# Both cross attentions regrouped: one tile of 128 queries at a time, probabilities packed end to end, next tile's scores issued first

## The chip, the cores and the metric

One kernel runs on one core of a Trainium2 chip. The metric is device time in microseconds (us), the median of several runs. The core's engines work in parallel, each through its own list of instructions in order, and wait for each other by semaphores: TensorE (PE; PEld are its weight loads), VectorE (DVE), ScalarE (ACT), GpSimd (POOL) and SyncE (SP, which issues transfers).

## The reference

Six blocks run in a row on 2048 tokens of 256 features (8 batches of 256), each followed by a residual and a layer norm: windowed self attention, cross attention, a routed feed-forward block, a recurrence, a second cross attention, a feed-forward block with binarized weights. The change touches the two cross attentions, which compute, for 16 heads of 16 features and 77 context rows per batch:

```
Q = proj(query, Wq, bq); K = proj(key, Wk, bk); V = proj(value, Wv, bv)
scores = jnp.einsum('bhqd,bhkd->bhqk', Q, K) / np.sqrt(D_K)
scores = jnp.where(m == 0, NEG, scores)      # the first; the second adds a mask
attn = jax.nn.softmax(scores, axis=-1)
x = jnp.einsum('bhqk,bhkd->bhqd', attn, V)
return x.transpose(0, 2, 1, 3).reshape(b, -1, D_MODEL) @ Wo.T + bo
```

## The kernel before, in words

`cross_attention` is called twice. The first call ("additive" false) gets an integer mask and the second ("additive" true) one to be added. A batch is two tiles of 128 queries, and a tile is cut into four units of four heads, so a batch has eight units. A loop in which each engine writes out its order by hand runs over the batches; the function `batch` of each engine is that order.

A unit goes through these steps. `score` (TensorE, L1200) is one f32 product of queries with a block of masked keys `ca_km`, 308 wide (4 heads x 77). `mask_scores` (VectorE, L1076 in the first call, L1074 in the second) writes the masked scores to `ca_z`. `take_maximum` (VectorE, L1082) finds the row maxima, `subtract` (GpSimd, L953) takes them off, `power` (ScalarE, L1017) is one exponential over 308. `turn_probs` (TensorE, L1209) transposes four blocks of 77, the copy to `ca_pth` (ScalarE, L1025) and `probs_rest` to `ca_ptl` (VectorE, L1087) split them into a high and a low f16 part. `weigh` (TensorE, L1223) is 12 small f16 products with the values, whose last column is the sum of the probabilities.

VectorE masks and reduces unit c+2 while it makes the low part of unit c, and ScalarE's exponential is for unit c+1. So three units are under way at once, each in one of two buffers:

```
L1110  two_on = (b, c + 2) if c < UNITS - 2 else (b + 1, c + 2 - UNITS) if after else None
L1112      mask_scores(*two_on)
L1113  probs_rest(b, c)
L1115      take_maximum(*two_on)
```

The other work of a batch (token transposes, the query, key and value projections of the next batch, head transposes, the output projection "mix") goes through two shared PSUM banks in a fixed ring, `CA`; its list of slots says after which unit each step stands. The 77 keys are masked by head on GpSimd (L947).

Of the kernel before, what the change touches and what calls it, by code (L numbers as in the profile page):

```python
# [209 lines left out]
def window_attention(nc, x_dram, xt_dram, wqkv_dram, wo_dram, rope_dram, ident, half, X, next_loads):  # L210
    with ExitStack() as ctx:
# [562 lines left out]
UH = 4  # L774
UNITS = TPB * CH // UH
MASKED = -4.0e9
OPEN = 1.0e38
CA = Ring(
    steps=[
        [("key", 0)],  # L780
        [("value", 0)],
        [("heads", 1)],
        [("mix", 1)],
        [("tokens", 0)],
        [("query", 0)],
        [("heads", 0)],
        [("mix", 0)],
    ],
# [6 lines left out]
class CrossWeights:  # L795


    def __init__(self, ctx, nc, tag, additive):
        self.tag, self.additive = tag, additive

        def sb(name, shape, dt=F32):
            return ctx.enter_context(nc.sbuf_tensor(f"{tag}_{name}", shape, dt))

        self.w = sb("w", [P, 4, KT_, DIM])
        self.bias = sb("bias", [P, 2, KT_])
        self.rows = sb("rows", [P, 2, DIM])
        self.mask = sb("mask", [P, TILES, CTX], F32 if additive else I32)
        self.loaded = ctx.enter_context(nc.semaphore(f"{tag}_loaded"))

    def load(self, sp, w_dram, b_dram, rows_dram, mask_dram):  # L810
        for tile, dram in ((self.bias, b_dram), (self.rows, rows_dram), (self.w, w_dram), (self.mask, mask_dram)):
# [3 lines left out]
def cross_attention(nc, weights, ctx_dram, ident, half, X, next_loads=None, table=None):  # L815
    tag, additive = weights.tag, weights.additive
    w, bias, rows, mask = weights.w, weights.bias, weights.rows, weights.mask
    with ExitStack() as ctx:
# [9 lines left out]
        context = [sb(f"context{k}", [P, KT_, CTX]) for k in range(2)]  # L828
        xs = [sb(f"xs{k}", [P, TPB, DIM]) for k in range(2)]
        limit = None if additive else sb("limit", [P, TILES, CTX])  # L830
        head_of = sb("head_of", [P, CH // KT_])
        xt = [sb(f"xt{k}", [P, KT_, SEQ]) for k in range(2)]
        q = [sb(f"q{k}", [P, KT_, SEQ]) for k in range(2)]
        kb = sb("kb", [P, KT_, CTX])
        km = [sb(f"km{k}", [P, KT_, CH // KT_, CTX]) for k in range(2)]
        v = sb("v", [P, CH, CD])
        vh = [sb(f"vh{k}", [P, CH, CD + 1], F16) for k in range(2)]
        vl = [sb(f"vl{k}", [P, CH, CD + 1], F16) for k in range(2)]
        z = [sb(f"z{k}", [P, UH, CTX]) for k in range(2)]
        top = sb("top", [P, 2, UH])  # L840
        probs = [sb(f"probs{k}", [P, UH, CTX]) for k in range(2)]
        pth = [sb(f"pth{k}", [P, UH * P], F16) for k in range(2)]
        ptl = [sb(f"ptl{k}", [P, UH * P], F16) for k in range(2)]
# [3 lines left out]
        xb = sb("xb", [P, TPB, DIM])  # L847

        shared = [ctx.enter_context(nc.psum_tensor(f"{tag}_shared{k}", [P, 512], F32)) for k in range(2)]
        s_bank = [ctx.enter_context(nc.psum_tensor(f"{tag}_scores{k}", [P, 512], F32)) for k in range(2)]  # L850
        t_bank = [ctx.enter_context(nc.psum_tensor(f"{tag}_turned{k}", [P, 512], F32)) for k in range(2)]
        o_bank = [ctx.enter_context(nc.psum_tensor(f"{tag}_out{k}", [P, CH, 32], F32)) for k in range(2)]
# [5 lines left out]
        limits = sem("limits")  # L858
        ones = sem("ones")
        full = [sem("full0"), sem("full1")]  # L860
        free = [sem("free0"), sem("free1")]
        key_masked = sem("key_masked")
# [11 lines left out]
        weighted = sem("weighted")  # L874
        inverted = sem("inverted")
        normed = sem("normed")
# [18 lines left out]

        block_scope = ExitStack()
# [3 lines left out]
        def _(sp):  # L900
            def load_context(b, par):
                sp.dma_start(context[par][:], ctx_dram[:, :, bass.ds(b * CTX, CTX)]).then_inc(context_loaded[par], 16)
# [28 lines left out]
        def _(pool):  # L931
# [8 lines left out]
            pool.wait_ge(consts, 3)  # L940
            if table:
                table.prepare(pool)
            pool.wait_ge(weights.loaded, 64)

            def mask_keys(b, par, g):
                wait_read(pool, [("key", 0)], b)
                pool.tensor_tensor(km[par][:, g], kb[:, g].unsqueeze(1).broadcast_to((P, CH // KT_, CTX)),  # L947
                                   head_of[:].unsqueeze(2).broadcast_to((P, CH // KT_, CTX)), ALU.mult).then_inc(key_masked, 1)
# [1880 lines left out]
```

## Time and profile before

| what | value |
|---|---|
| runs | 1293.85 us median of 3 (1289.38 to 1293.98) |
| profiled execution | 1291.09 us, of which the span of the core is 1289.3 us |
| mean granted TensorE clock | 0.924 of full speed |
| PE, DVE, ACT, POOL busy | 84%, 75%, 55%, 30% of the span |
| first cross attention | about 421 to 591.5 us of the span |
| second cross attention | about 1042 to 1207.7 us |

Busy time is a share of an engine's own time; PE's is modelled and its instructions overlap, so a busy PE isn't one at its peak. An idle time in square brackets on a row names what the engine waited for. A granted clock of 1.00 is 2.4 GHz, 0.50 is 1.2 GHz, and a mean between them is a stretch with some of both.

### The profile page before, as it was taken

What the parts mean: (1) busy time and instruction counts of PE and PEld (TensorE: products, weight loads), DVE (VectorE), ACT (ScalarE), POOL (GpSimd) and SP (SyncE); (2) the same over time, 40 slices, a digit from 0 to 9 for tenths busy, and PEclk for the clock granted to TensorE, in tenths of its full rate; (3) what the DMA queues carried; (4) which work ended last, traced back from release to release, by engine and by line L of the source; (5) the groups of instructions that cost most, each with busy time, mean ns of one, the idle gap of its engine ahead of it and who ended that gap; (6) DMA issues with size and microseconds to landing.
All of it is one profiled execution on the core that took longest, in us unless ns stands there. A gap on an engine that the chain in (4) does not pass through costs nothing. (4 is left out here: it accounts for less than half of the span.)

```text
span 1289.3 us, 30260 instructions
## 1 busy us (share of the span) xinstructions
PE 1087.8 (84%) x10763; PEld 881.4 (68%) x10763; DVE 961.6 (75%) x2254; ACT 704.9 (55%) x1459; POOL 388.9 (30%) x538
## 2 busy tenths in 40 slices
PE   4899989999987699986269999389999569999696
PEld 3578878778776577774257777378787447777485
DVE  7587877878875488884938883569998538888497
ACT  2454444444443355552637775368788525655484
POOL 5122222222220355551130000423331225555232
PEclk9899999999999799995559999699999879999799
DMA  6000000100000500005245431300000000000011
GB/s 257 5 10 2 10 12 2 71 3 2 2 2 2 187 23 22 11 9 227 107 135 172 171 108 49 120 17 26 24 9 9 0 24 23 11 21 9 34 50 50
DMA packets 34072, 65.35 MB, mean 51 GB/s; under 512 B 7590, under 2 KB 23334, under 8 KB 30886
## 3 DMA queue, kind: packets, MB, share of 16 engines
q1 hardware_dynamic: 32422, 59.62, 13.2%
q0 software_dynamic: 1536, 4.20, 1.0%
q8 instruction: 73, 1.20, 0.4%
q14 instruction: 41, 0.34, 0.1%
HBM read 43.03 MB, written 12.39 MB: 43 GB/s over the span
## 5 line engine op out<-in xcount | busy, mean ns | idle before, releaser
L953 POOL TENSOR_TENSOR ca_z<-ca_z,ca_top 128x308 f32<-128x308 f32 x128 | 92.7, 724 | 129.8 <-DVE ca_top L1082 129.5
L389 ACT ACTIVATE wa_probs<-wa_scores,wa_minus_top 128x192 f32<-128x192 f32 x256 | 83.3, 437 | 80.6 <-DVE wa_minus_top L477 80.6
L1025 ACT ACTIVATE ca_pth<-ca_turned 77x512 f16<-77x512 f32 x128 | 75.9, 593 | 59.0 <-PE ca_turned L1209 58.4
L348 POOL TENSOR_TENSOR wa_q<-wa_by_cos,wa_by_sin 128x256 f32<-128x256 f32 x32 | 23.4, 732 | 266.3 <-DVE wa_by_sin L472 266.3
L1209 PE MATMUL ca_turned<-ident,ca_probs 128*77 128x128 f32 x512 | 84.1, 287 | 20.6 <-ACT ca_probs L1017 19.5
L400 ACT ACTIVATE wa_pth<-wa_turned 128x384 f16<-128x384 f32 x128 | 58.4, 506 | 73.5 <-PE wa_turned L696 73.5
L1200 PE MATMUL ca_scores<-ca_km,ca_q 128*128 128x308 f32 x256 | 89.6, 433 | 6.0 <-ACT ca_q L998 5.7
L1087 DVE SCALAR_TENSOR_TENSOR ca_ptl<-ca_turned,ca_pth 77x512 f16<-77x512 f32 x128 | 86.7, 677 | 2.6 <-ACT ca_pth L1025 2.6
L1017 ACT ACTIVATE ca_probs<-ca_z 128x308 f32<-128x308 f32 x128 | 58.2, 455 | 44.8 <-POOL ca_z L953 43.8
L621 PE MATMUL wa_scores<-wa_xh,wa_wh 128*128 128x256 f16 x256 | 70.5, 275 | 11.7 <-DVE wa_wl L456 9.7
L477 DVE TENSOR_REDUCE wa_minus_top<-wa_scores 128x2 f32<-128x384 f32 x128 | 62.3, 549 | 21.1 <-PE wa_scores L684 18.9
L696 PE MATMUL wa_turned<-ident,wa_probs 128*128 128x128 f32 x512 | 69.1, 277 | 9.4 <-DVE wa_ptl L525 5.4
L1209 PEld LDWEIGHTS ca_turned<-ident,ca_probs 128*77 128x77 f32 x512 | 56.0, 148 | 26.4 <-ACT ca_probs L1017 22.6
L525 DVE SCALAR_TENSOR_TENSOR wa_ptl<-wa_turned,wa_pth 128x384 f16<-128x384 f32 x128 | 65.0, 549 | 8.6 <-ACT wa_pth L400 8.6
L2385 PE MATMUL re_g<-re_convh,re_w_gh 128*128 128x256 f16 x256 | 69.8, 273 | 1.2 <-DVE re_convl L2280 1.2
L621 PE MATMUL wa_scores<-wa_xl,wa_wh 128*128 128x256 f16 x256 | 70.5, 275 | 0.0
L621 PE MATMUL wa_scores<-wa_xh,wa_wl 128*128 128x256 f16 x256 | 70.4, 275 | 0.0
L2385 PE MATMUL re_g<-re_convl,re_w_gh 128*128 128x256 f16 x256 | 69.8, 273 | 0.0
L2385 PE MATMUL re_g<-re_convh,re_w_gl 128*128 128x256 f16 x256 | 69.8, 273 | 0.0
L696 PEld LDWEIGHTS wa_turned<-ident,wa_probs 128*128 128x128 f32 x512 | 58.1, 142 | 16.4 <-issue 7.5
L2369 PE MATMUL re_in<-re_xt,re_w_in 128*128 128x256 f32 x256 | 61.6, 402 | 9.0 <-ACT re_xt L2150 9.0
L2369 PEld LDWEIGHTS re_in<-re_xt,re_w_in 128*128 128x128 f32 x256 | 51.0, 202 | 18.8 <-issue 7.2
(332 smaller groups left out, 3677.0 us busy)
## 6 DMA issues: line engine op xcount, KB each, us to landing
ex_stage<-in_ew SPq DMA_DIRECT2D x16, 1024.0 KB, 7.0
slots<-slots_zeros SPq DMA_DIRECT2D x10, 512.0 KB, 5.3
ca_xs<-tokens SPq DMA_DIRECT2D x16, 256.0 KB, 2.3
ex_xe<-slots SPq DMA_DIRECT2D x11, 320.0 KB, 3.3
slots<-ex_y SPq DMA_DIRECT2D x9, 320.0 KB
wa_x_stage<-in_xt SPq DMA_DIRECT2D x8, 256.0 KB, 3.0
tokens<-in_x SPq DMA_DIRECT2D x1, 2048.0 KB, 14.8
ca_w<-in_xw SPq DMA_DIRECT2D x2, 1024.0 KB, 5.6
```

The lines of the kernel that those rows point to most:

```text
L389: ins = act.activation(probs[2 * (u % 2) + t][:, h, t * WINDOW:t * WINDOW + SPAN], s_bank[i][:, t * SPAN:(t + 1) * SPAN], ACT.Exp, bias=mi ...
L477: dve.tensor_reduce(minus_top[:, g % 2, i], s_bank[i][:, 0:2 * SPAN].rearrange("p (t s) -> p t s", t=2), AX.X, ALU.max, negate=True).then_ ...
L525: dve.scalar_tensor_tensor(out=spans(ptl[k][:]), in0=spans(t_bank[h][:]), scalar=PSCALE, in1=spans(pth[k][:]), op0=ALU.mult, op1=ALU.subtr ...
L621: ins = pe.matmul(bank[:, a * SEQ:(a + 1) * SEQ], weight[:, k, cols], x[:, par, k], start=(m == 0), stop=(m == 3 * KT_ - 1))
L696: ins = pe.transpose(t_bank[h][:, j * SEQ + t * P:j * SEQ + (t + 1) * P], probs[2 * (u % 2) + t][:, h, j * P:(j + 1) * P], ident[:])
L953: pool.tensor_tensor(z[k][:], z[k][:], top[:, k].unsqueeze(2).broadcast_to((P, UH, CTX)), ALU.subtract).then_inc(shift, 1)
L1025: act.activation(pth[k][0:CTX], t_bank[k][0:CTX], ACT.Copy, scale=PSCALE).then_inc(probs_high, 1)
L1087: dve.scalar_tensor_tensor(out=ptl[k][0:CTX], in0=t_bank[k][0:CTX], scalar=PSCALE, in1=pth[k][0:CTX], op0=ALU.mult, op1=ALU.subtract).then ...
L1200: pe.matmul(s_bank[c % 2][:, 0:UH * CTX], q[par][:, g, t * P:(t + 1) * P], km[par][:, g, h:h + UH].rearrange("p h k -> p (h k)"), start=Tr ...
L1209: ins = pe.transpose(t_bank[k][0:CTX, h * P:(h + 1) * P], probs[k][:, h], ident[:])
L2369: ins = pe.matmul(i_bank[s % 2][:, k], w_in[:, g, m * P:(m + 1) * P], xt[:, g], start=(g == 0), stop=(g == KT_ - 1))
L2385: ins = pe.matmul(g_bank[m][:, k], w[:, j, cols], x[par][:, j], start=(n == 0), stop=(n == 3 * HT - 1))
```

## The change

A unit of work becomes a tile of 128 queries: all 16 heads' scores stand in four PSUM banks at once (four heads in each). The 16 x 77 = 1232 probabilities of a query are written end to end (`ca_probs`, 1280 wide) and turned in ten blocks of 128 in three sets (4, 4 and 2 blocks), so that a block holds parts of two or three heads. The values are laid out to fit: 25 entries of a block and a head, each masked by a table `owner`, so the value projection is 20 products over blocks of 128 context rows (the context is given three times in a row). `weigh` is 30 products into one shared bank. The keys are not masked by head on GpSimd any more: ScalarE writes each 16-feature half in turn (L1038, four copies of 77), and the score products use 32 rows of the array each (8 products, 154 wide). In the first call the mask enters on TensorE by four bf16 products with an identity (L1306); in the second VectorE adds it. The largest score is subtracted by VectorE (first call) or GpSimd (second) for banks 0 and 1 only; for banks 2 and 3 ScalarE subtracts it as a bias, in four exponentials of 77 each.

Each engine's `batch` is now a loop over two tiles. `nxt` is the next tile, whose scores and exponentials are worked on while the present tile is turned. The core of the diff:

```diff
 # ScalarE
+                for t in range(TPB):
+                    nxt = ahead(b, t, after)
+                    if t == 0:
+                        slot(0, b, par)
+                    high(b, t, 0)
+                    if nxt:
+                        power(*nxt, 0)
+                    slot(6 if t else 1, b, par)
+                    high(b, t, 1)
+                    if nxt:
+                        power(*nxt, 1)
+                    if t == 0:
+                        slot(2, b, par)
+                    high(b, t, 2)
+                    if nxt:
+                        power(*nxt, 2)
+                    if t == 0:
+                        slot(3, b, par)
+                    elif after:
+                        value_high(b + 1, 1 - par)
+                    if nxt:
+                        power(*nxt, 3)
...
+            def power(b, t, r):
+                if r < SUBTRACTED:
+                    act.wait_ge(shift, SUBTRACTED * tile + r + 1)
+                    act.activation(out, z[r][:], ACT.Exp).then_inc(exped, 1)
+                else:
+                    act.wait_ge(maxed, UNITS * tile + r + 1)
+                    for h in range(UH):
+                        ins = act.activation(out[:, h], src[:, h], ACT.Exp, bias=minus_top[:, t, r, h:h + 1])
...
 # VectorE
+                for t in range(TPB):
+                    if t == 1:
                         normalise(b, 0)
+                    elif before:
                         normalise(b - 1, 1)
+                    if before:
+                        norm.apply(dve, b - 1, t, at(X, (b - 1) * TPB + t))
+                    low(b, t, 0)
+                    if nxt:
+                        softmax(*nxt, 0)
+                    low(b, t, 1)
+                    if nxt:
+                        softmax(*nxt, 1)
+                    if t == 1:
+                        slot(7, b, par)
+                    low(b, t, 2)
+                    if nxt:
+                        softmax(*nxt, 2)
+                        softmax(*nxt, 3)
+                    if t == 1 and after:
                         value_low(b + 1, 1 - par)
+                    slot(8 if t else 4, b, par)
...
+            def softmax(b, t, r):
+                dve.wait_ge(scores, tile + 1)
+                if additive:
+                    dve.tensor_tensor(z[r][:], s, m, ALU.add).then_inc(masked, 1)
+                dve.tensor_reduce(minus_top[:, t, r], z[r][:] if additive else s, AX.X, ALU.max, negate=True).then_inc(maxed, 1)
+                if r < SUBTRACTED and not additive:
+                    dve.tensor_tensor(z[r][:], s, minus_top[:, t, r].unsqueeze(2).broadcast_to((P, UH, CTX)),
+                                      ALU.add).then_inc(shift, 1)
...
 # TensorE
+            def score(b, t, par):
+                if not (first(b) and t == 0):
+                    pe.wait_ge(masked if additive else exped, UNITS * tile)
...
+                for t in range(TPB):
+                    if nxt:
+                        score(*nxt, par if t == 0 else 1 - par)
+                    if t == 0:
+                        slot(0, b, par)
+                    turn(b, t, 0)
+                    slot(6 if t else 1, b, par)
+                    turn(b, t, 1)
+                    slot(7 if t else 2, b, par)
+                    turn(b, t, 2)
+                    if t == 0:
+                        slot(3, b, par)
+                    slot(8 if t else 4, b, par)
+                    slot(9 if t else 5, b, par)
```

The slots of the ring are: 0 tokens, 1 heads 1 (of the batch before), 2 query, 3 key, 4 mix 1 (of the batch before), 5 weigh 0, 6 heads 0, 7 value, 8 mix 0, 9 weigh 1. Tokens, query, key and value serve the next batch. A step waits until the bank of the step two before it is read, so weigh 0 waits for ScalarE's key copy.

Two places of the order in the first call's loop follow. `ca_pth` and `ca_ptl` are the high and low parts, `ca_ot` turned heads, `ca_q` queries, `ca_xt` turned tokens; REGISTER_ALU and ISA rows are loop counters.

ScalarE, in the middle of a batch, before:

```order
L1025 ACTIVATE ca_pth<-ca_turned 77x512
L1014 REGISTER_ALU
L1017 ACTIVATE ca_probs<-ca_z 128x308
L993 REGISTER_ALU
L995 ACTIVATE ca_xt<-ca_shared 128x512
L1025 ACTIVATE ca_pth<-ca_turned 77x512
L1014 REGISTER_ALU
L1017 ACTIVATE ca_probs<-ca_z 128x308
L998 ACTIVATE ca_q<-ca_shared,ca_bias 128x256 x2
```

The same engine at the start of tile 0 now:

```order
L1074 ACTIVATE ca_pth<-ca_turned 128x512
L1059 ISA
L1060 ACTIVATE ca_probs<-ca_z 128x308
L1041 ACTIVATE ca_ot<-ca_shared 128x256
L1071 REGISTER_ALU
L1074 ACTIVATE ca_pth<-ca_turned 128x512
L1059 REGISTER_ALU
L1060 ACTIVATE ca_probs<-ca_z 128x308
L1028 REGISTER_ALU
L1033 ACTIVATE ca_q<-ca_shared,ca_q_bias 128x256 x2
L1071 REGISTER_ALU
L1074 ACTIVATE ca_pth<-ca_turned 128x256
```

VectorE in the same place, before:

```order
L1076 TENSOR_TENSOR ca_z<-ca_scores,ca_limit 128x308
L1087 SCALAR_TENSOR_TENSOR ca_ptl<-ca_turned,ca_pth 77x512
L1082 TENSOR_REDUCE ca_top<-ca_z 128x4
L1062 SCALAR_TENSOR_TENSOR ca_vl<-ca_v,ca_vh 77x16x16
L1076 TENSOR_TENSOR ca_z<-ca_scores,ca_limit 128x308
L1087 SCALAR_TENSOR_TENSOR ca_ptl<-ca_turned,ca_pth 77x512
L1082 TENSOR_REDUCE ca_top<-ca_z 128x4
```

And VectorE now:

```order
L1167 SCALAR_TENSOR_TENSOR ca_ptl<-ca_turned,ca_pth 128x512
L1147 ISA
L1155 TENSOR_REDUCE ca_minus_top<-ca_scores 128x4
L1158 ISA
L1159 REGISTER_ALU
L1160 TENSOR_TENSOR ca_z<-ca_scores,ca_minus_top 128x308
L1166 REGISTER_ALU
L1167 SCALAR_TENSOR_TENSOR ca_ptl<-ca_turned,ca_pth 128x512
L1155 TENSOR_REDUCE ca_minus_top<-ca_scores 128x4
L1158 REGISTER_ALU
L1159 REGISTER_ALU
L1160 TENSOR_TENSOR ca_z<-ca_scores,ca_minus_top 128x308
```

Where the exponential of one unit stood between the high parts of two others, whose maxima had been made an engine's turn earlier, it now stands between two sets of the same tile, and needs the reduction and the subtraction that stand between the same two sets on VectorE.

TensorE, where the value projection stands, before (`ca_turned` are the transposes):

```order
L1209 MATMUL ca_turned<-ident,ca_probs 77x128 x4
L1200 MATMUL ca_scores<-ca_km,ca_q 128x308
L1179 MATMUL ca_shared<-ca_w,ca_context 77x256 x2
L1218 ISA
L1223 MATMUL ca_out<-ca_vh,ca_pth 128x17
```

And in tile 1 now:

```order
L1324 MATMUL ca_turned<-ident,ca_probs 128x128 x4
L1276 MATMUL ca_shared<-ca_w,ca_context 128x32 x2
L1276 MATMUL ca_shared<-ca_w,ca_context 128x48 x2
L1276 MATMUL ca_shared<-ca_w,ca_context 128x32 x2
L1276 MATMUL ca_shared<-ca_w,ca_context 128x48 x4
L1276 MATMUL ca_shared<-ca_w,ca_context 128x32 x2
L1276 MATMUL ca_shared<-ca_w,ca_context 128x48 x4
L1276 MATMUL ca_shared<-ca_w,ca_context 128x32 x4
L1321 REGISTER_ALU
L1324 MATMUL ca_turned<-ident,ca_probs 128x128 x2
```

Two value products became 20, and the turning of a tile's third set stands behind them.

## Rows read from the trace of the kernel before

**Rows 1.** Busy time of each engine by stretch, number of instructions in brackets.
```profile
core 0: us, PE busy (x) PEld busy (x) DVE busy (x) ACT busy (x) POOL busy (x), PEclk, DMA share, GB/s
420.80:591.50 170.70, 146.48 (x1440) 118.64 (x1440) 131.70 (x343) 87.59 (x192) 86.65 (x116) 0.94 0.14 47
462.15:498.87 36.72, 34.79 (x361) 28.62 (x360) 32.65 (x86) 21.92 (x49) 21.32 (x29) 1.00 0.07 21
1060.07:1096.82 36.75, 34.27 (x359) 27.97 (x357) 30.88 (x79) 22.07 (x48) 21.32 (x28) 1.00 0.07 20
```
**Rows 2.** Timeline of VectorE: start, duration, engine, line, operation [idle before].
```profile
462.15 0.41 DVE L1057 TENSOR_TENSOR ca_v<-ca_shared,ca_rows 77x256 f32<-77x256 f32 x1
...
472.15 0.48 DVE L1076 TENSOR_TENSOR ca_z<-ca_scores,ca_limit 128x308 f32<-128x308 f32 x1 [1.34 <-PE ca_scores L1200]
472.55 0.68 DVE L1087 SCALAR_TENSOR_TENSOR ca_ptl<-ca_turned,ca_pth 77x512 f16<-77x512 f32 x1
473.14 0.46 DVE L1082 TENSOR_REDUCE ca_top<-ca_z 128x4 f32<-128x308 f32 x1
473.52 0.46 DVE L1076 TENSOR_TENSOR ca_z<-ca_scores,ca_limit 128x308 f32<-128x308 f32 x1
...
498.87 0.41 DVE L1057 TENSOR_TENSOR ca_v<-ca_shared,ca_rows 77x256 f32<-77x256 f32 x1
```
**Rows 3.** Waits from 462.15 to 535.61 us: total, times, longest.
```profile
DVE ca_z L1076 <- PE ca_scores L1200: 6.8, 8, 1.4
```
**Rows 4.** Timeline, all engines: a unit alone, at the first call's start.
```profile
435.03 0.47 DVE L1082 TENSOR_REDUCE ca_top<-ca_z 128x4 f32<-128x308 f32 x1
...
435.58 0.70 POOL L953 TENSOR_TENSOR ca_z<-ca_z,ca_top 128x308 f32<-128x308 f32 x1 [6.15 <-DVE ca_top L1082]
...
436.31 0.46 ACT L1017 ACTIVATE ca_probs<-ca_z 128x308 f32<-128x308 f32 x1 [3.84 <-POOL ca_z L953]
...
436.83 1.14 PE L1209 MATMUL ca_turned<-ident,ca_probs 128*77 128x128 f32 x4 [3.29 <-ACT ca_probs L1017]
```
**Rows 5.** Timeline of ScalarE in a steady batch.
```profile
467.02 0.60 ACT L995 ACTIVATE ca_xt<-ca_shared 128x512 f32<-128x512 f32 x1
...
470.06 0.84 ACT L998 ACTIVATE ca_q<-ca_shared,ca_bias 128x256 f32<-128x256 f32 x2 [0.49 <-PE ca_shared L1169]
470.84 0.59 ACT L1025 ACTIVATE ca_pth<-ca_turned 77x512 f16<-77x512 f32 x1
471.33 0.45 ACT L1017 ACTIVATE ca_probs<-ca_z 128x308 f32<-128x308 f32 x1
472.15 0.39 ACT L1005 ACTIVATE ca_ot<-ca_shared 128x256 f32<-128x256 f32 x1 [0.38 <-PE ca_shared L1184]
...
477.16 0.54 ACT L1003 ACTIVATE ca_kb<-ca_shared,ca_bias 128x77 f32<-128x77 f32 x2 [0.51 <-PE ca_shared L1175]
```
**Rows 6.** Timeline of TensorE: window attention, then weight loads and transposes of a cross batch.
```profile
300.00 0.81 PE L678 MATMUL wa_scores<-wa_band,wa_ident_bf 128*128 128x384 bf16 x4
300.75 1.58 PE L684 MATMUL wa_scores<-wa_k,wa_q 32*128 32x192 f32 x32
302.26 0.20 PE L714 MATMUL wa_out<-wa_vh,wa_pth 128*128 128x65 f16 x1
...
302.97 0.19 PE L714 MATMUL wa_out<-wa_vh,wa_ptl 128*128 128x65 f16 x1
...
475.77 1.12 PEld L1175 LDWEIGHTS ca_shared<-ca_context,ca_w 128*128 128x128 f32 x8
...
479.35 0.64 PE L1209 MATMUL ca_turned<-ident,ca_probs 128*77 128x128 f32 x4
```
**Rows 7.** Stretches of 3 us at the starts of both calls, columns as in rows 1.
```profile
433.00:436.00 3.00, 0.54 (x3) 0.05 (x1) 2.86 (x6) 0.00 (x0) 0.42 (x1) 0.84 1.09 385
436.00:439.00 3.00, 2.17 (x8) 1.81 (x8) 0.39 (x1) 1.40 (x3) 0.98 (x2) 0.50 1.09 385
...
1054.00:1057.00 3.00, 1.33 (x10) 1.20 (x10) 1.31 (x4) 1.17 (x4) 1.40 (x2) 1.00 0.00 0
```

More of the change, by code:

```diff
@@ L773 @@
 CH, CD = 16, 16
[L774 to L777, printed above, removed]
+UNITS = 4
+UH = CH // UNITS
+ROWS_T = CH * CTX
+CHUNKS = -(-ROWS_T // P)
+FLAT = CHUNKS * P
+SETS = [(0, 4), (4, 8), (8, CHUNKS)]
+PAIR = 2 * CTX
+SUBTRACTED = 2
+MASKED = -1.0e30
+TOUCHED = [(P * c // CTX, min(P * (c + 1) - 1, ROWS_T - 1) // CTX + 1) for c in range(CHUNKS)]
+ENTRY = [sum(z - a for a, z in TOUCHED[:c]) for c in range(CHUNKS)]
+ENTRIES = sum(z - a for a, z in TOUCHED)
+ORDER = [8 * g + 2 * r + j for r in range(UNITS) for g in range(KT_) for j in range(2)]
 CA = Ring(
     steps=[
+        [("tokens", 0)],
+        [("heads", 1)],
+        [("query", 0)],
         [("key", 0)],
+        [("mix", 1)],
+        [("weigh", 0)],
+        [("heads", 0)],
         [("value", 0)],
[L782 to L786, printed above, removed]
         [("mix", 0)],
+        [("weigh", 1)],
     ],
@@ L894, in both, with ahead @@
             return run
+        def ahead(b, t, after):
+            return (b, 1) if t == 0 else (b + 1, 0) if after else None
         block_scope = ExitStack()
@@ L1019, in batch @@
[L1019 to L1033 removed]
+                act.wait_ge(v_masked, b + 1)
@@ L1106, in residual, with slot @@
                 norm.statistics(dve, b, t)
[L1108 to L1116 removed]
+            def slot(s, b, par):
+                for kind, i, bank, uses in CA.slot(s, b):
+                    if kind == "value":
+                        value(b + 1, 1 - par, bank, uses)
+                    if kind == "mix":
+                        residual(b + CA.serves(kind, i), i, bank, uses)
@@ L1117, in batch @@
+            def batch(b, par, before=True, after=True):
+                for t in range(TPB):
+                    nxt = ahead(b, t, after)
+                    if t == 1:
                         normalise(b, 0)
-                    if c == 1 and before:
+                    elif before:
                         normalise(b - 1, 1)
-                    for kind, i, bank, uses in CA.slot(c, b):
-                        if kind == "value":
-                            value(b + 1, 1 - par, bank, uses)
-                        if kind == "mix":
-                            residual(b + CA.serves(kind, i), i, bank, uses)
@@ new lines, in turn @@
+            def turn(b, t, i):
+                n = 6 * b + 3 * t + i
+                pe.wait_ge(exped, UNITS * (b * TPB + t) + (2 if i == 0 else UNITS))
+                if not (first(b) and 3 * t + i < 2):
+                    pe.wait_ge(probs_low, n - 1)
+                a, e = SETS[i]
+                for c in range(a, e):
+                    ins = pe.transpose(t_bank[(3 * t + i) % 2][:, (c - a) * P:(c - a + 1) * P], probs[t][:, c * P:(c + 1) * P], ident[:])
+                ins.then_inc(probs_t, 1)
```

392 lines of the change are left out of this document (199 added, 193 removed).

## The prediction

> **What bounds the kernel now.** I read the busy times by stretch first. A steady stretch of two batches of either call, 36.7 us, has the clock at 1.00, and no engine but VectorE and TensorE is over 60% busy [rows 1]. The timeline of VectorE then shows the period: the same instruction (the value copy, L1057) starts at 462.15 and, two batches on, at 498.87, so a batch takes 18.36 us [rows 2]. Within it a unit's three VectorE steps start 0.40, 0.59 and 0.38 us apart, 1.37 us for mask, low part and maximum; the reader is to see that they follow each other without a gap, since each serves another unit. Eight units are 11.0 us of the 18.4; the rest is norms, copies and 1.7 us a batch of waiting for scores (6.8 us in four batches [rows 3]). So VectorE bounds both calls, and everything else runs beside it.
>
> The other view is one unit alone, at the start, where nothing overlaps [rows 4]: maximum, subtraction, exponential, transposes, each begun 0.03 to 0.08 us after the one before has ended. Before the change that chain is hidden by the three units under way. I call such a step a hand-off and take 0.05 us.
>
> **What the change takes off VectorE.** In the first call, per tile, four masks (0.40 each) go, two subtractions come (0.48, with 0.04 of waiting for the maximum ahead), and the low parts fall from four of 512 to two of 512 and one of 256 (0.60 + 0.60 + 0.33 = 1.53 for 2.4). Per tile 4 x 1.37 = 5.5 becomes two maxima with subtraction (2 x 0.89), two without (2 x 0.38) and 1.53: 4.1. In the second call each maximum must wait for its own add right ahead of it (0.52 + 0.38), so 4 x 0.90 + 1.53 = 5.1. With the wait for scores gone too, VectorE alone would allow 18.36 - 1.7 - 2.8 = 13.9 and 18.36 - 1.7 - 0.8 = 15.9 us a batch. That is the gain on offer: 4.5 and 2.5 us a batch.
>
> **What the change adds: a chain between ScalarE and VectorE.** Both engines take their lists in order. ScalarE's list reads: high part of set 0, exponential 0 of the next tile, high part of set 1, exponential 1, high part of set 2, exponentials 2 and 3. VectorE's reads: low part 0, maximum 0 (and subtraction), low part 1, maximum 1, low part 2, maxima 2 and 3. Low part 0 needs high part 0; maximum 0 stands behind low part 0; exponential 0 needs maximum 0; high part 1 stands behind exponential 0; and so on. While one works the other waits, where before every step's input had been made a unit earlier. I add up one tile from the end of high part 0 to the same point of the next tile. Durations: copy of 512 starts its follower 0.49 after it and lasts 0.59, exponential of 308 0.45, query copies 0.74 to the next start, head copy 0.30 to the next (0.39 long), token copy 0.52, two copies of 77 with a bias 0.54, so 0.22 apart and 0.32 long [rows 5]. Four pieces of 77 are then 0.98, or 0.88 to the next start; a 256-wide f16 copy I take as the 256-wide head copy, 0.38.
>
> First call. Round 0: hand-off 0.05, low 0.60, maximum 0.46 and 0.04, subtraction 0.48, hand-off 0.05, exponential 0.45, head copy 0.30, high part 0.59: 3.0. Round 1: the same with high part 0.38 and no head copy, 2.5, in tile 0 with the query copies 3.25. Round 2: 0.05, low 0.33, maximum 0.46, 0.05, pieces 0.88, key copies 0.88 (tile 0) or value copy 0.45 (tile 1), pieces 0.98: 3.65 and 3.2. Then the turn-round, since here the next scores wait for the last exponential, and the transposes stand behind the scores. A score step is four bf16 products of 308 (four of 384 start 0.16 apart, so 0.13 each) and 16 short-row products (8 f32 ones, each shown as two; 32 of 192 wide take 1.58, 0.04 each): 0.52 + 0.64 and 0.3 until the last is out, 1.46, of which the transposes wait for 1.2 [rows 6]. Transposes 0.64, hand-off, high part 0.59: with the score a little late behind weigh 0 it is 2.6 after tile 0; after tile 1, where the token transposes (0.65) and their copy (0.52) come first, 3.1. Tile 0 is 12.5, tile 1 is 11.8.
>
> In tile 1 the value projection stands ahead of set 2's transposes: 20 products, 40 weight loads. Eight such loads take 1.12, 0.13 apart [rows 6], so 5.2 us for what took four. It starts about when high part 0 ends, so high part 2 ends at 5.2 + 0.40 + 0.05 + 0.38 = 6.0 where the rounds alone give 5.5: 0.4 more. A batch of the first call is 24.7 us, 6.3 over 18.36.
>
> Second call. Rounds 0 and 1 have the add (0.52) and GpSimd's subtraction (0.70 [rows 4], 0.72 with hand-off part) in place of VectorE's subtraction: 3.8 and 3.3 (4.0 with the query). Round 2: 4.15 and 3.7. The next scores wait only for the adds, and so run early. But weigh 0 (30 f16 products at 0.03 [rows 6], 0.93) waits for the key copies, and scores (0.64) and transposes (0.64) stand behind it: 2.0. After tile 1 the token transposes wait for the residual, behind the value's low part on VectorE: 1.85. Tiles 14.0 and 12.65; a batch 26.6, 8.3 over 18.36.
>
> **The sum.** Seven batch periods lie within each call: 7 x 6.3 = 44 and 7 x 8.3 = 58. At the ends, the first value projection has 36 more loads ahead of the first scores (36 x 0.13 = 4.7, up to 8 at half clock), the context transfer is three times as large, and the last tile lacks a next tile's rounds; I take +2 a call, between -3 and +8. That is +106.
>
> The rest is TensorE's clock. In tile 0, after the key projection, TensorE has only the mix products (about 1 us) until the key copies: by the rounds above it is silent for some 2.4 and 2.0 us in the first call, 3.1 and 2.5 in the second. At the first call's start it was silent for 3.29 us [rows 4], and the granted clock fell to 0.84 and 0.50 in those stretches; in the stretch of 1054 us, with 1.33 us of work in three, it stayed at 1.00 [rows 7]. So it may fall in some batches. At half rate the pieces on the chain cost themselves once more: 1.2 + 0.64 + 0.9 = 2.7 us a batch in the first call, 0.93 + 0.64 + 0.64 = 2.2 in the second, and some 2 for the value projection. Nothing in any batch is 0, all batches of both calls 7 x (2.7 + 2.2 + 2) = 48; I take 10, since only the second call's silences come near 3.29.
>
> The profiled execution took 1291.1 us (span 1289.3 and 1.8 around it), 2.8 below the median of the runs. 1291 + 106 + 10 = 1407.
>
> The Trainium skill ("TensorE: Matmul & The Clock Gate", section "What's actually happening") says that the default state is throttled and that activity releases the throttle. By that rule a stage with such holes would lose the clock in every batch, and the sum would be 1445; the row of 1054 us speaks against counting on it. The same skill ("TensorEngine Tiling (Array Packing)", section "Key Properties") says that a change of tiling mode drains the engine, which speaks against short-row products twice a batch. The trace shows the first of them 0.27 us after the last full-height product started at 0.16 us a step [rows 6]; by the rule with that number it is 0.11 x 4 a batch at most, already within the 0.3 above.
>
> **Rivals.** (a) The same chain, and the clock falls in nearly every batch: 1291 + 106 + 48 = 1445. For it: the holes; against it: the row of 1054 us. (b) The pieces of the chain are cheaper than the rows of before allow to see, above all ScalarE's exponentials of 77 and the copies beside them, so that half of the excess goes: 1291 + 53 + 10 = 1354. For it: those shapes have no row of their own; against it: 0.22 apart is what copies with a bias show. (c) Faster: VectorE stays the bound. It decides from where ScalarE's high parts and exponentials are ready before VectorE reaches them, so that the rounds overlap; then 7 x (4.5 + 2.5) = 49 goes and some 6 comes at the ends, 1248. For it: VectorE has the largest share now and is given less to do; against it: the order of the two lists, which leaves no step that could be early. (d) No net change: in the first call VectorE bounds (-32), in the second half of the excess comes (+29): 1288. That the four exponentials run at all and the sets are as wide as said is in the order.
>
> **How the numbers follow.** The forecast has 0.62, (a) 0.18, (b) 0.10, (c) 0.06, (d) 0.04. A difference under 0.5% can't be told from none here. Faster 0.06, same 0.04, slower 0.90. The range goes from 1350, just past (b), to 1445, which takes in (a); what lies outside is (c), (d) and the tails, some 0.15. The likeliest case's own range is 1385 to 1425.
>
> **What would show it.** The period between value copies on VectorE: 24.7 and 26.6 us a batch. ScalarE idle before its exponentials, released by VectorE's (second call: GpSimd's) subtraction, and VectorE idle before its low parts, released by ScalarE's high part, about 0.6 us and more each, six or so times a tile; VectorE under 65% busy in both calls. The value projection about 5 us at the full clock. The prediction is wrong if VectorE has no idle time before its low parts, if the period is under 21 us, or if the time is gained back outside both calls, where nothing changes.

## The result, and the profile after

| | time, us | ratio to before (95% interval) | profiled execution | clock |
|---|---|---|---|---|
| before | 1293.91 median of 4 | | 1291.09 | 0.924 |
| after | 1454.1 median of 4 (1453.88 to 1459.07) | 1.1243 (1.1190 to 1.1296) | 1453.88, span 1451.9 | 0.849 |

12% slower. The direction and the mechanism came out as forecast, the size did not: 1454 against 1407, 9 us above the upper end of the range. All of the difference but 2.6 us lies in the two cross attentions. From the first context transfer to the last residual they took 167.4 and 164.1 us before and take 241.3 and 250.2 now, +160.0.

First the counterpart of [rows 1]: a batch of the first call and one of the second, from value copy to value copy (us, busy us and instructions of each engine, granted clock, DMA share, GB/s).

```profile
529.92:557.24 27.32, 20.96 (x194) 17.07 (x193) 13.97 (x38) 11.73 (x36) 3.89 (x7) 0.81 0.06 18
1253.02:1282.94 29.92, 22.10 (x182) 19.17 (x181) 15.83 (x41) 12.27 (x36) 6.78 (x10) 0.69 0.05 17
```

Five of the six steady batches of the first call take 27.3 us and one 25.9 (mean 27.1), instead of 18.36 [rows 2]; in the second call the six take 29.4 in the mean (28.1 to 32.1). VectorE is busy 51 to 53% of a batch, where it had 84 to 89%, and the clock, at 1.00 in [rows 1], is 0.81 and 0.69.

The waits of two batches (529.92 to 584.56), the counterpart of [rows 3], and of two of the second call (1253.02 to 1311.07): engine and line, what it waited for, us in total, times, longest.

```profile
DVE ca_ptl L1167 <- ACT ca_pth L1074: 18.2, 12, 2.4
...
ACT ca_probs L1060 <- DVE ca_z L1160: 13.2, 8, 1.7
```

```profile
ACT ca_probs L1060 <- POOL ca_z L979: 19.8, 8, 2.8
DVE ca_ptl L1167 <- ACT ca_pth L1074: 19.1, 11, 2.3
```

These are the two sides of the alternation: VectorE waits before all twelve low parts for ScalarE's high part, and ScalarE before all eight whole exponentials for the subtraction. VectorE's timeline in one tile shows it [idle before, and for whom]:

```profile
566.12 0.69 DVE L1167 SCALAR_TENSOR_TENSOR ca_ptl<-ca_turned,ca_pth 128x512 f16<-128x512 f32 x1 [2.29 <-ACT ca_pth L1074]
566.72 0.47 DVE L1155 TENSOR_REDUCE ca_minus_top<-ca_scores 128x4 f32<-128x308 f32 x1
567.23 0.48 DVE L1160 TENSOR_TENSOR ca_z<-ca_scores,ca_minus_top 128x308 f32<-128x308 f32 x1
568.99 0.69 DVE L1167 SCALAR_TENSOR_TENSOR ca_ptl<-ca_turned,ca_pth 128x512 f16<-128x512 f32 x1 [1.28 <-ACT ca_pth L1074]
...
572.11 0.42 DVE L1167 SCALAR_TENSOR_TENSOR ca_ptl<-ca_turned,ca_pth 128x256 f16<-128x256 f32 x1 [1.53 <-ACT ca_pth L1074]
```

From one low part to the next is 2.87 and 3.12 us; round 0 was forecast at 3.0 and round 1 with the query at 3.25. The reader sees rounds of the forecast length, in batches that are 2.6 us too long. The rest stands in the clock. Stretches of 2 us of the same tile (PE's busy time is the second number, the clock the third from the end):

```profile
558.00:560.00 2.00, 1.21 (x32) 0.83 (x30) 1.20 (x3) 1.12 (x6) 0.91 (x1) 1.00 0.46 118
560.00:562.00 2.00, 0.65 (x3) 0.41 (x4) 1.51 (x5) 1.22 (x5) 0.00 (x0) 0.87 0.00 0
562.00:564.00 2.00, 2.00 (x19) 1.29 (x18) 1.65 (x4) 0.00 (x0) 1.43 (x3) 0.50 0.00 0
564.00:566.00 2.00, 2.00 (x15) 2.00 (x15) 0.00 (x0) 1.11 (x2) 0.00 (x0) 0.78 0.00 0
...
570.00:572.00 2.00, 0.14 (x1) 0.15 (x1) 0.55 (x2) 1.39 (x4) 0.00 (x0) 0.93 0.00 0
572.00:574.00 2.00, 1.93 (x4) 1.02 (x4) 1.23 (x4) 1.12 (x6) 0.00 (x0) 0.50 0.00 0
```

The clock falls twice in the batch: at 561, after the weighing of tile 1, and at 572, after the key projection. TensorE's timeline shows what then runs at half rate:

```profile
561.35 1.11 PE L1306 MATMUL ca_scores<-ca_mask_now,ca_ident_bf 128*128 128x308 bf16 x4 [1.82 <-ACT ca_probs L1065]
562.40 1.41 PE L1312 MATMUL ca_scores<-ca_km,ca_q 32*128 32x154 f32 x16
563.73 1.11 PE L1258 MATMUL ca_shared<-ident,ca_xs 128*128 128x128 f32 x4
...
571.86 2.07 PE L1288 MATMUL ca_shared<-ca_w,ca_ot 128*128 128x256 f32 x4 [2.21 <-ACT ca_q L1033]
```

At full clock (e1_fill below) the first three take 0.69, 0.81 and 0.66, the last 1.03 to 1.13. So the batch spends 1.5 us more before the next high part 0 and 1.0 more before the weighing, 2.5 of the 2.6 us.

At the first call's start, the counterpart of [rows 7], the value projection is the long row, and the clock is 0.50 although TensorE is shown busy without a break:

```profile
425.07 1.96 PE L1270 MATMUL ca_shared<-ca_context,ca_w 128*128 128x77 f32 x8 [6.63 <-DMA ca_context<-in_context]
426.82 8.66 PE L1276 MATMUL ca_shared<-ca_w,ca_context 128*128 128x32 f32 x40
```

```profile
427.00:430.00 3.00, 3.00 (x17) 3.00 (x16) 0.00 (x0) 1.33 (x4) 0.00 (x0) 0.50 1.08 385
430.00:433.00 3.00, 3.00 (x16) 3.00 (x16) 0.00 (x0) 0.00 (x0) 0.00 (x0) 0.50 1.08 382
```

### The profile page after: what moved, and what is told of

The parts are those of the page before. It is cut to its first block and busy times, and to the rows that moved or that the text cites. A ratio compares the mean times of both kernels' runs of the same rounds, so it can differ in the third digit from the quotient of the medians.

```text
span 1451.9 us, 30374 instructions
## 1 busy us (share of the span) xinstructions
PE 1162.0 (80%) x10891; PEld 951.6 (66%) x10891; DVE 944.9 (65%) x2201; ACT 721.8 (50%) x1651; POOL 300.1 (21%) x444
## 5 line engine op out<-in xcount | busy, mean ns | idle before, releaser
L1167 DVE SCALAR_TENSOR_TENSOR ca_ptl<-ca_turned,ca_pth 128x512 f16<-128x512 f32 (+1 forms) x96 | 57.6, 602 | 149.1 <-ACT ca_pth L1074 149.1
L1060 ACT ACTIVATE ca_probs<-ca_z 128x308 f32<-128x308 f32 x64 | 29.4, 460 | 130.2 <-POOL ca_z L979 73.4
L1276 PEld LDWEIGHTS ca_shared<-ca_w,ca_context 128*128 128x128 f32 x640 | 93.2, 236 | 0.0
L1276 PE MATMUL ca_shared<-ca_w,ca_context 128*128 128x32 f32 (+1 forms) x640 | 92.9, 313 | 0.0
L1288 PE MATMUL ca_shared<-ca_w,ca_ot 128*128 128x256 f32 x128 | 52.4, 552 | 34.8 <-ACT ca_q L1033 30.2
L1074 ACT ACTIVATE ca_pth<-ca_turned 128x512 f16<-128x512 f32 (+1 forms) x96 | 49.8, 520 | 58.0 <-PE ca_turned L1324 58.0
L1246 PEld LDWEIGHTS ca_shared<-ca_vh,ca_pth 128*128 128x128 f16 x320 | 31.9, 109 | 54.3 <-issue 37.0
L1246 PE MATMUL ca_shared<-ca_vh,ca_pth 128*128 128x34 f16 (+1 forms) x320 | 35.1, 200 | 40.0 <-ACT ca_km L1038 22.5
```

Source lines behind the costliest of these rows:

```text
L1167: dve.scalar_tensor_tensor(out=ptl[t][:, a * P:e * P], in0=t_bank[(3 * t + i) % 2][:, 0:(e - a) * P], scalar=PSCALE, in1=pth[t][:, a * P:e ...
L1246: ins = pe.matmul(out, p[:, cols], x[:, ENTRY[c]:ENTRY[c] + e - a].rearrange("p e d -> p (e d)"), start=(c == 0 and n == 0), stop=(c == CH ...
L1276: ins = pe.matmul(dst[:, ENTRY[c] * CD:(ENTRY[c] + e - a) * CD], context[par][:, k, key:key + P], w[:, 2, k, a * CD:e * CD], start=(k == 0 ...
L1288: ins = pe.matmul(dst[:, 0:DIM], ot[:, i, g], w[:, 3, g], start=(g == 0), stop=(g == KT_ - 1))
```

## The experiments

Calls are measured from the first context transfer to the last residual, batches between value copies (mean of the six behind the first interval), both in the profiled execution. The rest of the program takes 957 to 962 us in all kernels but e7.

| kernel | time, us | ratio (95% interval) | calls, us | batch, us |
|---|---|---|---|---|
| after | 1454.1 | 1.1243 (1.119 to 1.130) | 241.3, 250.2 | 27.1, 29.4 |
| e1_fill | 1428.3 | 1.1005 (1.095 to 1.106) | 225.4, 237.0 | 25.0, 27.4 |
| e2_high | 1433.0 | 1.1041 (1.100 to 1.108) | 234.3, 239.4 | 26.9, 27.7 |
| e3_turn | 1448.9 | 1.1164 (1.103 to 1.129) | 238.0, 244.0 | 27.2, 27.6 |
| e4_value | 1470.2 | 1.1328 (1.128 to 1.137) | 248.6, 262.4 | 28.8, 30.8 |
| e5_order | 1297.0 | 1.0008 (0.999 to 1.003) | 166.0, 169.3 | 18.0, 17.9 |
| e6_mixed | 1429.0 | 1.1031 (1.098 to 1.109) | 228.7, 238.9 | 25.5, 27.1 |
| e7_value8 | 1436.8 | 1.1091 (1.104 to 1.115) | 241.6, 249.8 | 27.8, 29.3 |
| e8_shift | 1266.1 | 0.9759 (0.970 to 0.981) | 150.7, 154.6 | 16.7, 17.0 |
| e9_shift_warm | 1271.8 | 0.9815 (0.977 to 0.986) | 150.9, 154.9 | 16.6, 17.0 |
| e10_first8 | 1440.8 | 1.1114 (1.100 to 1.123) | 234.4, 244.1 | 27.1, 29.6 |

**e1_fill: idle transposes in TensorE's holes.**

```diff
+            def fill(n, b, t):
+                pe.wait_ge(probs_low, 6 * b + 3 * t + 2)
+                for _ in range(n):
+                    pe.transpose(t_bank[(3 * t + 1) % 2][:, 0:P], ident[:], ident[:])
 # after the key projection 14, after mix 1 of tile 0 12, after weigh 1 10;
 # 40 once, ahead of the first batch
```

> The changed kernel with idle TensorE transposes of the identity added, into a transpose bank that nothing uses at that moment: 14 after the key projection, 12 after mix 1, 10 after weigh 1 in each batch and 40 before the first batch (0.11 us each at full clock). They add no result. If the excess over the forecast (1454 against 1407) is TensorE's clock, the granted clock in steady batches rises from 0.81 and 0.69 to 0.95 or more, the periods fall from 27.3 and 29.4 us to 24.7 and 26.6 as forecast, and the time to 1400 to 1415. If instead the pieces of the chain between ScalarE and VectorE were sized too small, the clock rises and the periods stay above 26.5 and 28.5: 1440 or more.

1428.3, 26 less than the changed kernel, between the two expectations. Both of the falls seen above went; one at a new place stayed in most batches. The last batch of the first call had none, and the one of 545 did (one stretch is the value projection itself):

```profile
545.90:550.90 5.00, 5.00 (x48) 5.00 (x46) 3.01 (x6) 1.82 (x4) 0.00 (x0) 1.00 0.00 0
550.90:552.90 2.00, 2.00 (x14) 1.39 (x13) 1.68 (x5) 0.98 (x4) 1.03 (x1) 0.51 0.21 25
...
600.50:625.00 24.50, 21.38 (x231) 18.45 (x230) 14.34 (x38) 11.67 (x36) 3.90 (x7) 1.00 0.00 0
```

A batch wholly at full clock takes 24.5 us; 24.7 was forecast. And the clock fell at 551 at the end of 4.55 us of value products, with no idle time on TensorE since 543. The same 4.55 us of products in the last batch left it at 1.00, so they alone do not decide it:

```profile
546.29 4.55 PE L1276 MATMUL ca_shared<-ca_w,ca_context 128*128 128x32 f32 x40
...
620.34 4.55 PE L1276 MATMUL ca_shared<-ca_w,ca_context 128*128 128x32 f32 x40
```

**e2_high: ScalarE makes high part 1 ahead of exponential 0.**

```diff
                     high(b, t, 0)
+                    high(b, t, 1)
                     if nxt:
                         power(*nxt, 0)
                     slot(6 if t else 1, b, par)
-                    high(b, t, 1)
```

> The changed kernel with one swap on ScalarE: the high part of set 1 stands ahead of exponential 0 instead of behind it. If the alternation of ScalarE and VectorE is the chain, this takes the high part (0.59), the exponential (0.45), the head copy (0.30) and two hand-offs out of it, 1.3 to 1.4 us a tile over 32 tiles: 1454 - 43 = 1411, and VectorE's idle time before low part 1 goes. If TensorE's steps (scores, turning, value projection at the low clock) set the period, the time stays within 10 us of 1454.

1433.0, half of the gain expected. In two batches of the first call the wait before low parts fell from 18.2 to 14.0 us and that before exponentials from 13.2 to 6.6, so one hand-off less a tile does what it should; but ScalarE's wait for the transposes rose from 7.1 to 13.1, and the clock takes a share. Two batches of the second call, one after the other:

```profile
1211.60:1236.80 25.20, 18.91 (x186) 16.45 (x186) 15.55 (x40) 12.53 (x36) 6.30 (x9) 0.87 0.03 10
1236.80:1266.40 29.60, 23.49 (x185) 20.97 (x184) 15.77 (x41) 12.62 (x36) 6.29 (x9) 0.71 0.08 26
```

The same instructions in the same order, 4.4 us apart, with the clock at 0.87 and 0.71.

**e3_turn: TensorE turns set 0 ahead of the next tile's scores.**

```diff
+                    turn(b, t, 0)
                     if nxt:
                         score(*nxt, par if t == 0 else 1 - par)
                     if t == 0:
                         slot(0, b, par)
-                    turn(b, t, 0)
```

> The changed kernel with set 0 of a tile turned ahead of the next tile's scores instead of behind them. Chain theory: the high and low part of set 0 (1.2 us) then run beside the scores instead of behind them, and the scores are 1.2 us at the full clock, 2.4 at half: 1 to 2 us a tile in the first call, 0.6 in the second, 16 tiles each: 1454 - 26 to 42, so 1412 to 1428. Rival (the order of the two steps on TensorE does not matter, since the next maxima need the scores in either order): 1447 to 1461.

1448.9 (1442.2, the run that the table's calls are from, and 1455.6); the interval holds the changed kernel's ratio, so no gain can be told. The first call's period stays at 27.2, so the turn-round alone isn't what bounds it there; presumably a high part made earlier meets the same alternation.

**e4_value: the value projection behind set 2's transposes** (VectorE's and ScalarE's value steps moved behind it).

```diff
-                    slot(7 if t else 2, b, par)
+                    if t == 0:
+                        slot(2, b, par)
                     turn(b, t, 2)
+                    if t == 1:
+                        slot(7, b, par)
```

> The changed kernel with the value projection behind set 2's transposes on TensorE, its copy behind maximum 3 on VectorE and the high part of the values behind exponential 3 on ScalarE. The forecast gave the value projection 0.4 us a batch of the first call (8 batches, 3 us) by holding up set 2; the trace of the changed kernel shows set 2's high part beginning right behind exponential 1, so this should bring 0 to 10 us: 1444 to 1454. Rival: 40 weight loads at the low clock (8.6 us) hold up set 2 in every batch; then 2 to 3 us a batch, 1405 to 1425.

1470.2: slower by 16, where both expectations were of no loss. The projection now stands between set 2 and the weighing, the clock of the steady batches is 0.67 to 0.74, and ScalarE's longest wait for transposes is 4.2 us (3.6 without the edit). Where the projection stood it cost less; what of the 16 us is the clock and what the place is not told apart.

**e5_order: the same instructions, another order within the tile, on all four engines.** The lists of three engines for tile 0, in words (GpSimd's and those of tile 1 change too):

```diff
 # ScalarE
-tokens, high 0, exp 0, heads, high 1, exp 1, query, high 2, exp 2, key, exp 3
+high 0, tokens, heads, high 1, key, exp 0, high 2, exp 1, query, exp 2, exp 3
 # VectorE
-norm, apply, low 0, max 0, low 1, max 1, low 2, max 2, max 3, residual
+norm, low 0, max 0, max 1, max 2, low 1, low 2, apply, max 3, residual
 # TensorE
-score, tokens, turn 0, heads, turn 1, query, turn 2, key, mix, weigh
+turn 0, tokens, score, heads, turn 1, key, turn 2, query, mix, weigh
```

> Same instructions on every engine, only their order within a tile is changed, on all four: ScalarE makes the high parts of sets 0 and 1 before the next tile's exponentials, VectorE takes three of the next maxima between its low parts, TensorE turns set 0 first and runs the key projection ahead of the query. Theory (the alternation of the two lists is the excess): VectorE alone needs 13.9 and 15.9 us a batch, TensorE's pieces add up to 17.2 in the first call (value 5.0, scores 2.4, transposes 2.5, mix 1.75, query 1.75, weigh 1.9, key 0.95, tokens and heads 1.0) and 16.0 in the second, so TensorE and VectorE bound it: periods of 17.5 to 18.5 and 16.8 to 17.5 at full clock, 1300 us; with a clock that still falls once a batch 2 to 3 us more, 1340. Rival (the clock, not the order, makes most of the excess): the holes move but stay, 1400 or more. Rival (the rounds' length is in the pieces themselves): periods stay over 24 and the time over 1425.

1297.0, the time of the kernel before: the order of the four lists was worth 157 us, what it spared in falls of the clock included. Two batches of the first call and two of the second, and the wait before low parts in the two from 485.4 to 520.6:

```profile
502.90:538.10 35.20, 33.62 (x386) 28.89 (x385) 27.54 (x72) 23.54 (x72) 8.39 (x14) 1.00 0.09 28
1084.13:1119.83 35.70, 34.48 (x369) 30.45 (x368) 30.81 (x82) 24.42 (x73) 13.37 (x18) 0.88 0.10 31
```

```profile
DVE ca_ptl L1183 <- ACT ca_pth L1081: 2.3, 4, 0.7
```

2.3 us where it was 18.2, and in the first call VectorE 78% and TensorE 96% busy at clock 1.00. TensorE is the engine that is full now. Both rivals fall: at clock 1.00 the old order still takes 24.5 us a batch (e1_fill), the new one 17.6; in the second call the new order takes 17.9 though the clock still falls (0.88). Four lists changed at once, so which swap counts most is not told; one swap on ScalarE alone (e2_high) was worth 21 us, one on TensorE alone (e3_turn) nothing that can be told.

**e6_mixed: e1_fill, with two idle transposes after each of the value projection's last blocks.**

```diff
+                        if c == 2 and not first(b):
+                            pe.wait_ge(probs_low, 6 * b - 2)
+                        if 2 <= c < len(TOUCHED) - 1:
+                            for _ in range(2):
+                                pe.transpose(t_bank[1][:, 0:P], ident[:], ident[:])
```

> The kernel of e1_fill, and beside it two idle transposes after each of the last blocks of the value projection (14 in all, some 1.7 us a batch). In e1_fill the clock still fell once a batch, at the end of the value projection, where TensorE has no idle time in the trace. Theory (a stream of small products behind weight loads lowers the clock by itself): with wide products among them the clock stays at 1.00 in the steady batches, periods are 24.7 plus about 1 in the first call and 26.6 plus 1 in the second, and the time 1415 to 1430, since what the clock gives back the transposes take. Rival (the fall comes from a silence elsewhere): the granted clock of the steady batches stays at 0.9 and the time rises by 14 x 1.7 to about 1450.

The clock stays at 1.00 through all six steady batches of either call; four of each:

```profile
526.30:577.30 51.00, 45.29 (x487) 39.43 (x486) 28.45 (x73) 23.58 (x72) 7.81 (x14) 1.00 0.06 20
577.30:628.20 50.90, 45.18 (x486) 39.35 (x485) 28.44 (x73) 23.57 (x72) 7.83 (x14) 1.00 0.03 10
1181.10:1235.60 54.50, 43.23 (x470) 38.17 (x469) 31.47 (x80) 24.41 (x72) 12.49 (x19) 1.00 0.06 20
1235.60:1290.10 54.50, 43.24 (x470) 38.18 (x469) 31.49 (x80) 24.40 (x72) 12.49 (x19) 1.00 0.06 18
```

Against e1_fill the only edit is inside the value projection, so the unbroken stream of small products had a part in the falls there; that it is not enough by itself the last batch of e1_fill shows. The projection is 1.2 us longer (5.75 for 4.55) and the batch 0.95 longer than e1_fill's at full clock, so the time stays.

**e7_value8: the value projection of batches 1 to 7 in 4 wide products.**

```diff
+                    for lo, hi in () if first(b) else ((0, DIM), (DIM, ENTRIES * CD)):
+                        for k in range(KT_):
+                            ins = pe.matmul(dst[:, lo:hi], context[par][:, k, 0:P], w[:, 2, k, 0:hi - lo],
+                                            start=(k == 0), stop=(k == KT_ - 1))
-                    for c, (a, e) in enumerate(TOUCHED):
+                    for c, (a, e) in enumerate(TOUCHED if first(b) else ()):
```

> The changed kernel with the value projection of batches 1 to 7 done in 4 wide products (8 weight loads, columns 256 and 144) instead of 20 small ones (40 loads); left out is each block's own offset into the context, so the values are not the reference's. The forecast has 0.4 us a batch of the 5.2 us projection on the path at full clock: by that alone 14 x 0.4 = 6, 1448. If the projection also causes the fall of the clock at the end of tile 1, that fall goes, the scores and transposes after tile 1 are back at full rate (some 2 us a batch), and the time is 1415 to 1430. If the silence around the weighing of tile 1 causes that fall, it stays, and the time is 1440 to 1450.

The 17 us that it is faster lie between the calls, 14 of them in the feed-forward block that routes by the data (942 us outside the calls instead of 960). The calls themselves did not change. With the products gone TensorE is silent there and the clock falls all the same, from 1.00 to 0.50:

```profile
582.00:584.00 2.00, 0.00 (x0) 0.00 (x0) 1.65 (x5) 0.73 (x2) 0.67 (x1) 0.91 0.12 42
584.00:586.00 2.00, 1.27 (x30) 1.16 (x30) 0.92 (x3) 1.58 (x7) 0.36 (x1) 0.50 0.00 0
```

So the projection is only one cause of the falls, and neither its length nor its loads bound the steady batch with the clock as it was; with the clock held at 1.00 this was not tried.

**e8_shift: e5_order, with the value projection done once on 77 rows and moved into its ten blocks by f16 products, and the order fitted to it again.** ScalarE makes `v_hi`, VectorE `v_lo`; `pick` is the identity of 77 three times over. The new order is left out here.

```diff
+                    for k in range(KT_):
+                        ins = pe.matmul(dst[0:CTX, DIM:2 * DIM], context[par][:, k, 0:CTX], w[:, 2, k],
+                                        start=(k == 0), stop=(k == KT_ - 1))
 # value
-                        for k in range(KT_):
-                            ins = pe.matmul(dst[...], context[par][:, k, key:key + P], w[:, 2, k, a * CD:e * CD], ...)
+                        for n, x in enumerate((v_hi, v_lo)):
+                            ins = pe.matmul(dst[...], pick[0:CTX, key:key + P], x[0:CTX, a * CD:e * CD], ...)
```

> The reordered kernel of e5_order, and the value projection done once per batch on 77 rows (4 products beside the key projection, 8 weight loads), split in two f16 parts (ScalarE 0.35, VectorE 0.35 us), and moved into its ten blocks by 20 f16 products with a repeated identity (0.03 apart, 0.6 us) instead of 20 f32 products with 40 weight loads (4.6 at full, 8.7 us at half clock); the order within a tile is fitted to this again. TensorE's pieces fall from 17.2 to 13.6 us in the first call and from 16.0 to 12.4 in the second; VectorE then bounds, 14.3 and 16.3. Theory (in e5_order TensorE bounds, and the first value projection of each call costs some 6 us more at half clock): periods 15.7 to 16.8 and 16.3 to 17.3 instead of 17.8 and 17.9, so 7 x 1.5 + 7 x 1.1 = 18, and 2 x 6 at the starts: 1267, between 1255 and 1285. Rival (the clock falls more often with less work on TensorE and takes the gain): 1285 to 1300. Rival (the ends don't come from the value projection): the starts stay as long, 1275 to 1285.

1266.1 us, faster than both kernels: 0.976 of before, with an interval (0.970 to 0.981) that leaves open whether it is by 2%. Two batches of each call:

```profile
486.10:519.60 33.50, 28.78 (x356) 22.24 (x356) 28.38 (x75) 22.90 (x74) 8.30 (x14) 1.00 0.10 31
1087.60:1120.70 33.10, 26.85 (x339) 21.07 (x338) 31.50 (x84) 24.57 (x74) 13.03 (x18) 1.00 0.10 31
```

VectorE is busy 85 and 95% again. That is 28 of the 49 us, 7 x (4.5 + 2.5), that the forecast saw on offer: the batches are 16.7 and 17.0 us, where it had VectorE alone allow 13.9 and 15.9. What of the 31 us against e5_order is the projection and what the order fitted again is not told apart.

**e9_shift_warm: 20 idle transposes at each call's start.**

```diff
+            for _ in range(20):
+                pe.transpose(t_bank[0][:, 0:P], ident[:], ident[:])
```

> e8_shift with 20 idle transposes of the identity at the start of each call, while the context is on its way (TensorE is silent there for 6.6 and 8.1 us in e5_order, and its first products run at half clock). If the silence sets the clock of the call's start, the first pieces (key 1.96 instead of 1.1, tokens, query, scores, transposes) come back to full rate: 2 to 5 us a call, 4 to 10 less than e8_shift. If the clock falls again at once behind them, no difference (within 4 us).

No gain: the calls agree with e8_shift's within 0.3 us, and the two intervals overlap. In the first call the idle transposes hold TensorE until 428.1, so the key projection starts 6.7 us after the first transfer (3.1 in e8_shift). It and the value products then run at full rate (1.01 and 1.03 us for 1.96 and 1.91). The first value copy comes 1.8 us later after the transfer (11.6 for 9.8), the first batch is 1.3 us shorter (18.81 for 20.15), so the edit takes back what it gives.

**e10_first8: only the first value projection of each call in 4 wide products** (e7's edit, the other way round).

> The changed kernel with only the first value projection of each call done in 4 wide products (8 weight loads) instead of 20 small ones; left out is each block's own offset into the context, so the values of batch 0 are not the reference's (the stage between the calls, whose work goes by the data, may change its length; read are the two calls, 241.3 and 250.2 us from the first context transfer to the last residual). If the 8.66 us of the first projection at half clock is what the ends cost over the forecast, the first value copy comes 6 to 7 us earlier and both calls are 6 to 7 us shorter, 13 together. If the start is bound by something beside it (the first exponentials, the half clock of all that follows), the calls are shorter by less than 3 us each.

Both calls are shorter, by 6.9 and 6.1 us, as the first theory says (the first value copy comes 5.5 us earlier, a little less than expected). The row that was 8.66 us is now:

```profile
424.92 2.96 PE L1275 MATMUL ca_shared<-ca_w,ca_context 128*128 128x256 f32 x8
```

## Why the prediction was wrong, step by step

- **What bounds, and the alternation: right.** VectorE went from bound to half idle, with the waits in the named pairs; e5_order shows by experiment that the excess over before, falls of the clock included, came from the order of the lists. The gain on offer did not come with it, since TensorE was then full.
- **The rounds: right.** Forecast 24.7 us a batch in the first call; 24.5 at full clock (e1_fill). In the second 26.6; measured 27.1 with the transposes of e6_mixed inside, which cost 0.95 in the first call; without them it wasn't measured. One piece was too small: the key copies, with a scale and a bias from tables, take 1.31 to 1.35 us for four, not 0.98. One reading was off by 0.04: what follows the query copies starts 0.78 us after them [rows 5], not 0.74.
- **The value projection beside the rounds: right, as far as tested.** 0.4 us a batch on the path, for 5.2 us of projection; it takes 4.55 at full clock, and e7_value8 took away 32 of 40 loads and gained nothing in the calls.
- **The clock term: the step that failed.** "Nothing in any batch is 0, all batches of both calls 7 x (2.7 + 2.2 + 2) = 48; I take 10, since only the second call's silences come near 3.29." It fell twice in the batch shown, and stretches of 30 us have 0.79 to 0.83 in the first call (500 to 650 us) and 0.66 to 0.85 in the second (1170 to 1350). Its price: 27.1 - 24.5 = 2.6 a batch in the first call, at least 29.4 - 27.1 = 2.3 in the second, 7 x 4.9 = 34, or 41 if e6's transposes cost 0.95 in the second call too. The upper bound of 48 was sized well; the 10 chosen within it was wrong, by 24 to 31 of the 47 us that the forecast missed. It rested on one row of before, 1.33 us of work in 3 at clock 1.00 [rows 7]. After the change 1.21 and then 0.65 in 2 us were followed by a fall. One row with the clock up was no measure of a loop that repeats the hole twice a batch. The fall after tile 1 was not foreseen at all: its silence was only 1.82 us, with the value stream and the weighing's small products ahead of it. The Trainium skill ("TensorE: Matmul & The Clock Gate", section "What's actually happening") says that throttled is the default and activity releases it; by that rule the forecast had 1445. The traces after agree in that the clock fell in every steady batch; they also show it at 0.50 through 8.66 us that the profile shows as busy, which that sentence by itself would not give.
- **The ends: too small, and outside their bounds.** "I take +2 a call, between -3 and +8." 241.3 - 167.4 - 7 x 8.72 = +13 and 250.2 - 164.1 - 7 x 11.06 = +9. 13 of these 22 are the first value projections (e10_first8): forecast with "4.7, up to 8 at half clock", they take 8.66 at half clock for 1.9 before, 6.8 more, and no other engine has much to do beside them. So they are within what was said of them, 2 us a call over the 4.7, and most of the 18 us missed here lies elsewhere. The first interval between value copies is long in both calls (41.2 and 34.2 us), and in the first the clock is 0.58 in it; how much of that is the clock no run tells:

```profile
435.53:476.71 41.18, 29.09 (x183) 23.79 (x183) 11.84 (x26) 13.36 (x39) 3.27 (x7) 0.58 0.20 64
```

The sum with the measured terms: 1291 + 7 x (24.5 - 18.36) + 7 x (26.2 - 18.37) + 41 + 22 + 2.6 outside the calls = 1454, with 26.2 for the second call as e6's 27.1 less 0.95, an inference. It is an account and no test: the price of the clock and the ends are what the measured times leave over, so it closes by construction. Against the forecast the rounds are 4 us less, the clock up to 31 more, the ends 18 more and the rest 2.6 more. Of the rivals (a) came nearest, and it lacked the ends.

## What to carry to other kernels

Two in-order engines that hand each tile's pieces to each other in turn can cost nearly the sum of both, however idle each is (here 14.0 and 11.7 us busy in a batch of 27.3): count hand-offs per list before you count busy time, and try another order of the same instructions before another algorithm. Where a change opens holes of some 2 us on TensorE twice a batch, as here, take the half-clock price as a term of the sum, in every batch, until a row of a loop with such holes shows otherwise. Price the first batch apart, with nothing to hide behind and the clock low.

## What the runs showed of the hardware

TensorE's clock fell behind, or stayed low under, work that the profile shows as unbroken. In e1_fill it fell at 551 us at the end of 4.55 us of f32 products 32 and 48 columns wide, each behind a load of 128 columns, without idle time since 543; with two 128-wide transposes after most of the blocks (e6_mixed) it stayed at 1.00. The same products in the last batch of that call of e1_fill left it at 1.00 too. At the call's start it stayed at 0.50 through 8.66 us of them. What decides between these, and whether the short columns or the loads matter, was not tried apart.
